# A graph-network layer in fp32 on one core: tile 1 turned on TensorE, HT_hi and HT_lo doubled, and the first tiles reordered

## What is computed

```python
h = jnp.maximum(_layernorm(x, axis=-1), 0.0)                    # x: 50000 x 256
agg = segment_sum(edge_attr_64, dst, 50000)                     # 25000 edges x 64, dst sorted
agg = agg / jnp.maximum(counts, 1.0)[:, None]
combined = jnp.concatenate([agg, h], axis=1)                    # 50000 x 320
out = x + relu(combined @ W1 + b1) @ W2 + b2                    # W1 320 x 512, W2 512 x 256
```

## Time and profile before

| | |
|---|---|
| median of 3 runs | 1362.57 us (1361.99 to 1363.06) |
| the profiled execution's own time | 1361.83 us |
| its span | 1360.0 us |
| busy: TensorE products | 1333.9 us (98%) |
| busy: VectorE | 1194.1 us (88%) |
| busy: ScalarE | 695.4 us (51%) |
| busy: POOL | 539.7 us (40%) |
| chain that ended last | TensorE 95%, VectorE 3%, DMA 1%, POOL 1% |

### The profile page before, as it was taken

One profiled execution on the slowest core, in us unless ns is written; L12 is line 12 of the kernel. 1 busy time (PEld: TensorE's weight loads), 2 busy tenths in 40 slices (PEclk: granted clock), 3 DMA queues, 4 the chain that ended last, 5 costly groups with the idle time before them and its releaser, 6 DMA issues.

```text
span 1360.0 us, 29811 instructions
## 1 busy us (share of the span) xinstructions
PE 1333.9 (98%) x7066; PEld 1118.8 (82%) x7066; DVE 1194.1 (88%) x2961; ACT 695.4 (51%) x1281; POOL 539.7 (40%) x710
## 2 busy tenths in 40 slices
PE   4899999999999999999999999999999999999999
PEld 2688888888888888888888888888888888888887
DVE  5989898988888898989898989898889888989897
ACT  3445555555555454545454545454545454545553
POOL 6333343434343434343434343434343434343431
PEclk9999999999999999999999999999999999999999
DMA  4455555555454545454545464545454545555542
GB/s 112 111 127 120 133 121 130 126 126 130 121 132 120 132 120 133 119 136 115 140 112 143 109 147 107 145 108 143 111 141 112 139 114 137 116 135 118 133 111 74
DMA packets 422724, 168.59 MB, mean 124 GB/s; under 512 B 321188, under 2 KB 422326, under 8 KB 422712
## 3 DMA queue, kind: packets, MB, share of 16 engines
q1 hardware_dynamic: 421720, 167.28, 51.2%
q10 hardware_dynamic: 992, 1.18, 0.3%
HBM read 66.12 MB, written 51.40 MB: 86 GB/s over the span
## 4 chain that ended last, share of the span: by engine, by line
PE 95%; DVE 3%; DMA 1%; POOL 1%; issue 0%; ACT 0%; POOLq 0%; DVEq 0%; SPq 0%
PE P L907 26%; PE P L909 13%; PE P L884 13%; PE P L886 13%; PE P L885 13%; PE P L893 6%; PE P L894 6%; PE PA L873 2%; PE PA L874 2%; DVE H_lo L715 0%; DMA dst_w<-in_dst_dram 0%; DVE OH L813 0%; DVE below L670 0%; DVE stats L645 0%; DVE HT L699 0%
## 5 line engine op out<-in xcount | busy, mean ns | idle before, releaser
L907 PE MATMUL P<-w_both,H_hi 128*128 128x512 f32 x1564 | 557.6, 397 | 1.1 <-DVE H_lo L715 1.0
L596 ACT ACTIVATE H_hi<-P 128x512 fp32r<-128x512 f32 x392 | 233.1, 596 | 513.4 <-PE P L894 513.4
L909 PE MATMUL P<-w_both,H_lo 128*128 128x256 f32 x1564 | 439.6, 281 | 0.0
L715 DVE SCALAR_TENSOR_TENSOR H_lo<-P,H_hi 128x512 fp32r<-128x512 f32 x392 | 268.0, 685 | 113.2 <-ACT H_hi L596 103.2
L907 PEld LDWEIGHTS P<-w_both,H_hi 128*128 128x128 f32 x1564 | 293.7, 188 | 74.8 <-DVE H_lo L715 3.4
L884 PE MATMUL P<-HT_hi,w_hi 128*128 128x512 f32 (+1 forms) x784 | 314.4, 401 | 1.9 <-ACT w_both L610 1.9
L886 PE MATMUL P<-HT_hi,w_lo 128*128 128x512 f32 (+1 forms) x784 | 308.9, 394 | 0.0
L885 PE MATMUL P<-HT_lo,w_hi 128*128 128x512 f32 (+1 forms) x784 | 306.0, 390 | 0.0
L909 PEld LDWEIGHTS P<-w_both,H_lo 128*128 128x128 f32 x1564 | 293.4, 188 | 3.7
L438 POOL TENSOR_TENSOR XB<-X,b_row 128x1024 f32<-128x1024 f32 x98 | 236.8, 2416 | 135.5 <-DVE O L729 135.3
L432 POOL TENSOR_TENSOR E_lo<-ES,E_hi 128x256 fp32r<-128x256 f32 x98 | 73.2, 747 | 400.6 <-ACT E_hi L576 400.6
(11 more groups left out here) (74 smaller groups left out, 1140.0 us busy)
## 6 DMA issues: line engine op xcount, KB each, us to landing
HQ<-HN SPq DMA_DIRECT2D x388, 128.0 KB, 3.1
out_dram<-O SPq DMA_DIRECT2D x97, 512.0 KB, 3.3
X<-in_x_dram SPq DMA_DIRECT2D x96, 512.0 KB, 3.6
ER<-in_edge_attr_dram SPq DMA_DIRECT2D x392, 32.0 KB, 1.8
DT<-table_dram SPq DMA_DIRECT2D x392, 1.0 KB, 1.7
X<-in_x_dram ACTq DMA_DIRECT2D x1, 512.0 KB, 5.0
w_raw<-in_L_gnn_W_dram ACTq DMA_DIRECT2D x4, 128.0 KB, 5.2
w_raw<-in_L_gnn_W_dram SPq DMA_DIRECT2D x2, 256.0 KB, 4.0
```

Of the source, the lines that this page charges most:

```text
L596: act.activation(H1_hi[:, m, nodes(t)], bank(m)[:, nodes(t)], ACT.Relu).then_inc(s_1hi, 1)
L715: dve.scalar_tensor_tensor(out=H1_lo[:, m, nodes(t)], in0=bank(m)[:, nodes(t)], scalar=0.0, in1=H1_hi[:, m, nodes(t)], op0=ALU.max, op1=AL ...
L907: pe.matmul(out_bank(j)[some, :], H1_hi[:, m, rows], w2_both[:, m, :, :].rearrange("p a d -> p (a d)"), start=(m == 0), stop=False)
L909: last = pe.matmul(out_bank(j)[some, 0:D], H1_lo[:, m, rows], w2_both[:, m, 0, :], start=False, stop=(m == CH - 1))
```

## The change

Tile 1 is turned as tile 0 is: TensorE transposes HN of tile 1 into the P2 banks, and SP's move and VectorE's transposes of tile 1 are gone. HT_hi and HT_lo have two buffers, taken by turns. The first-layer products of tile 0 have another order: all w1_hi x HT_hi, then the transposes of tile 1, all w1_lo x HT_hi, the edge means, all w1_hi x HT_lo. POOL computes norm(1) directly behind w1_lo, the parts wb_lo behind the flag's test, norm(2) behind the low part of w2, and each XB of tiles 1, 2 and 3 behind that tile's edges and behind a new wait for its one-hots (`s_oh`). ScalarE normalizes tile 1 ahead of the split of w2 and makes HT_hi of tile 1 ahead of tile 0's means. VectorE tests the flag before `transposed_low(0)` and the statistics of tile 2; the one-hots of tile 3 come before the residuals of tile 1, and `means_low(2)` after the first of them. In `moved` the count of moves is adapted.

```diff
@@ -141,4 +141,4 @@
         HT = sb("HT", [P, CD, TILE])
-        HT_hi = sb("HT_hi", [P, CD, TILE], F32R)
-        HT_lo = sb("HT_lo", [P, CD, TILE], F32R)
+        HT_hi = [sb(f"HT_hi{b}", [P, CD, TILE], F32R) for b in range(2)]
+        HT_lo = [sb(f"HT_lo{b}", [P, CD, TILE], F32R) for b in range(2)]
         QA = sb("QA", [P, TILE], F32R)
@@ -194,3 +194,3 @@
 
-            return P2[c][:] if isinstance(t, int) and t == 0 else HT[:, c, :]
+            return P2[c][:] if isinstance(t, int) and t < 2 else HT[:, c, :]
 
@@ -268,4 +268,4 @@
             if isinstance(t, int):
-                return MOVED * (t // 2 + b)
-            return MOVED // 2 * t + MOVED // 2 * b
+                return MOVED * (t // 2)
+            return MOVED // 2 * t - MOVED // 2 * b
 
@@ -382,3 +382,2 @@
             load_windows(1, 1)
-            move(1, 1)
             load_x(3, 1)
@@ -477,10 +476,3 @@
             pool.tensor_tensor(w1_lo[:], w1_raw[:], w1_hi[:], ALU.subtract).then_inc(s_wlo, 1)
-            pool.wait_ge(s_whi, 3)
-            pool.wait_ge(s_wlo, 1)
-            pool.tensor_tensor(wb_lo[0:DE, :], wa_raw[0:DE, :], wa_hi[0:DE, :], ALU.subtract).then_inc(s_wblo, 1)
-            pool.wait_ge(s_wblo, 1)
-            pool.tensor_tensor(wb_lo[96:P, :], b1_raw[96:P, :], b1_hi[96:P, :], ALU.subtract).then_inc(s_wblo, 1)
-            pool.wait_ge(s_wblo, 2)
             norm(1, 1)
-            norm(2, 0)
             pool.wait_ge(s_start, 1)
@@ -530,2 +522,7 @@
                     pool.wait_ge(s_gout, 16 * i + 16)
+            pool.wait_ge(s_whi, 3)
+            pool.tensor_tensor(wb_lo[0:DE, :], wa_raw[0:DE, :], wa_hi[0:DE, :], ALU.subtract).then_inc(s_wblo, 1)
+            pool.wait_ge(s_wblo, 1)
+            pool.tensor_tensor(wb_lo[96:P, :], b1_raw[96:P, :], b1_hi[96:P, :], ALU.subtract).then_inc(s_wblo, 1)
+            pool.wait_ge(s_wblo, 2)
             edges_scaled(0, 0)
@@ -534,7 +531,10 @@
             pool.tensor_tensor(w2_both[:, :, 1, :], w2_raw[:], w2_both[:, :, 0, :], ALU.subtract).then_inc(s_wlo, 1)
-            residual_in(1, 1)
+            norm(2, 0)
             edges_scaled(1, 1)
             edges_low(1, 1)
+            pool.wait_ge(s_oh, 2 * SUB)
+            residual_in(1, 1)
             edges_scaled(2, 0)
             edges_low(2, 0)
+            pool.wait_ge(s_oh, 3 * SUB)
             residual_in(2, 0)
@@ -543,2 +543,3 @@
             edges_low(3, 1)
+            pool.wait_ge(s_oh, 4 * SUB)
             residual_in(3, 1)
@@ -566,3 +567,3 @@
                     rows, into = X[b][:, j, :], HN[b][:, j, :]
-                    if isinstance(t, int) and t == 0:
+                    if isinstance(t, int) and t < 2:
                         rows = rows.rearrange("p (q c f) -> p q c f", q=QN, c=CD)
@@ -577,7 +578,7 @@
 
-            def transposed_high(t):
-                past(act, s_l1, CH * t)
+            def transposed_high(t, b):
+                past(act, s_l1, CH * (t - 1))
                 for c in range(CD):
                     act.wait_ge(s_th, 2 * t + c + 1)
-                    act.activation(HT_hi[:, c, :], turned(t, c), ACT.Copy).then_inc(s_hhi, 1)
+                    act.activation(HT_hi[b][:, c, :], turned(t, c), ACT.Copy).then_inc(s_hhi, 1)
 
@@ -607,7 +608,8 @@
             layernorm(0, 0)
-            transposed_high(0)
+            transposed_high(0, 0)
+            layernorm(1, 1)
             act.wait_ge(s_w[3], 32)
             act.activation(w2_both[:, :, 0, :], w2_raw[:], ACT.Copy).then_inc(s_whi, 1)
-            layernorm(1, 1)
             edges_high(0, 0)
+            transposed_high(1, 1)
             means_high(0)
@@ -616,3 +618,2 @@
             layernorm(2, 0)
-            transposed_high(1)
             means_high(1)
@@ -620,3 +621,3 @@
             hidden_high(1)
-            transposed_high(2)
+            transposed_high(2, 0)
             means_high(2)
@@ -627,3 +628,3 @@
                     hidden_high(2 * i + h)
-                    transposed_high(2 * i + (h + 1))
+                    transposed_high(2 * i + (h + 1), 1 - h)
                     means_high(2 * i + (h + 1))
@@ -632,3 +633,3 @@
             hidden_high(TILES - 2)
-            transposed_high(TILES - 1)
+            transposed_high(TILES - 1, 1)
             means_high(TILES - 1)
@@ -701,3 +702,3 @@
 
-            def transposed_low(t):
+            def transposed_low(t, b):
                 for c in range(CD):
@@ -705,4 +706,4 @@
                     if c == 0:
-                        past(dve, s_l1, CH * t)
-                    dve.tensor_tensor(HT_lo[:, c, :], turned(t, c), HT_hi[:, c, :], ALU.subtract).then_inc(s_hlo, 1)
+                        past(dve, s_l1, CH * (t - 1))
+                    dve.tensor_tensor(HT_lo[b][:, c, :], turned(t, c), HT_hi[b][:, c, :], ALU.subtract).then_inc(s_hlo, 1)
 
@@ -745,3 +746,3 @@
                     transpose(t + 1, 1 - b, 1)
-                    transposed_low(t + 1)
+                    transposed_low(t + 1, 1 - b)
                 if latest:
@@ -766,6 +767,3 @@
             stat(1, 1, range(SUB))
-            transposed_low(0)
             aggregate(1, 1)
-            stat(2, 0, range(SUB))
-            aggregate(2, 0)
             dve.wait_ge(s_start, 1)
@@ -816,4 +814,8 @@
             dve.wait_ge(s_const, 12)
+            transposed_low(0, 0)
+            stat(2, 0, range(SUB))
+            aggregate(2, 0)
             ends(0, 0)
             onehot(0, 0)
+            transposed_low(1, 1)
             means_low(0)
@@ -823,5 +825,2 @@
             onehot(1, 1)
-            transpose(1, 1, 0)
-            transpose(1, 1, 1)
-            transposed_low(1)
             means_low(1)
@@ -838,10 +837,9 @@
             transpose(2, 0, 1)
-            transposed_low(2)
-            residual(1, 1, 0)
-            residual(1, 1, 1)
-            means_low(2)
-            residual(1, 1, 2)
-            residual(1, 1, 3)
+            transposed_low(2, 0)
             ends(3, 1)
             onehot(3, 1)
+            residual(1, 1, 0)
+            means_low(2)
+            for j in range(1, SUB):
+                residual(1, 1, j)
             with dve.Fori(1, TILES // 2 - 1) as i:
@@ -876,3 +874,3 @@
 
-            def layer1_nodes(t, m):
+            def layer1_nodes(t, b, m):
                 if m == 0:
@@ -883,5 +881,5 @@
                 for c in range(CD):
-                    pe.matmul(bank(m)[:, nodes(t)], w1_hi[:, c, cols], HT_hi[:, c, nodes(t)], start=(c == 0), stop=False)
-                    pe.matmul(bank(m)[:, nodes(t)], w1_hi[:, c, cols], HT_lo[:, c, nodes(t)], start=False, stop=False)
-                    pe.matmul(bank(m)[:, nodes(t)], w1_lo[:, c, cols], HT_hi[:, c, nodes(t)], start=False, stop=False)
+                    pe.matmul(bank(m)[:, nodes(t)], w1_hi[:, c, cols], HT_hi[b][:, c, nodes(t)], start=(c == 0), stop=False)
+                    pe.matmul(bank(m)[:, nodes(t)], w1_hi[:, c, cols], HT_lo[b][:, c, nodes(t)], start=False, stop=False)
+                    pe.matmul(bank(m)[:, nodes(t)], w1_lo[:, c, cols], HT_hi[b][:, c, nodes(t)], start=False, stop=False)
 
@@ -918,3 +916,3 @@
                     if not (isinstance(t, int) and t == 0):
-                        layer1_nodes(t, m)
+                        layer1_nodes(t, b, m)
                     layer1_means(t, m)
@@ -922,2 +920,5 @@
                         edge_means(t + 1, 1 - b)
+                if isinstance(t, int) and t == 0:
+                    pe.wait_ge(s_whi, 5)
+                    pe.wait_ge(s_wlo, 2)
                 layer2(t)
@@ -927,8 +928,11 @@
             pe.wait_ge(s_const, 9)
-            for j in range(SUB):
-                pe.wait_ge(s_ln, j + 1)
-                for c in range(CD):
-                    last = pe.transpose(P2[c][:, j * P:(j + 1) * P], HN[0][:, j, c * P:(c + 1) * P], ident[:])
-                    if j == SUB - 1:
-                        last.then_inc(s_th, 1)
+            def turn(t):
+                for j in range(SUB):
+                    pe.wait_ge(s_ln, SUB * t + j + 1)
+                    for c in range(CD):
+                        last = pe.transpose(P2[c][:, j * P:(j + 1) * P], HN[t][:, j, c * P:(c + 1) * P], ident[:])
+                        if j == SUB - 1:
+                            last.then_inc(s_th, 1)
+
+            turn(0)
             with pe.If(flag != 0):
@@ -941,12 +945,18 @@
             pe.wait_ge(s_whi, 1)
+            for c in range(CD):
+                pe.wait_ge(s_hhi, c + 1)
+                for m in range(CH):
+                    pe.matmul(bank(m)[:], w1_hi[:, c, m * P:(m + 1) * P], HT_hi[0][:, c, :], start=(c == 0), stop=False)
+            pe.wait_ge(s_hlo, 2)
+            turn(1)
             pe.wait_ge(s_wlo, 1)
-            layer1_nodes(0, 0)
-            layer1_nodes(0, 1)
-            layer1_nodes(0, 2)
-            layer1_nodes(0, 3)
+            for c in range(CD):
+                for m in range(CH):
```

(6 more changed lines are left out.)

## The result

The changed kernel takes 1365.13 us (median of 13 runs, 1363.44 to 1366.32), the kernel before, run beside it, 1362.38 (13 runs, 1360.39 to 1364.74): a ratio of 1.0025, 95% interval [1.0017, 1.0033]. It is 2.75 us slower by the medians. The interval lies clear of 1, so it is a small loss, just above the 0.2% (2.7 us) that the prediction calls no difference. The profiled execution took 1366.23 us, with a span of 1364.6, and is near the slow end of its 13 runs.

A forecast was written before the change was run, and what follows sets the result against it. TensorE never waits in the steady loop, so only the first four tiles count. 0.4 us less and 1.6 more turn the profiled 1361.83 into 1363.0; from the median, 1362.57 + 1.2 = 1363.7, range 1357.0 to 1366.4.

The forecast's parts named there:

- The start: Up to S, when tile 0's means products begin on TensorE: S at 32.0 instead of 34.41, a gain of 2.4 us.
- XB(1), X(3), ES(2): POOL's XB(1) waits for one-hot(1) until 37, SP's X(3) goes out at 39.5, 2.8 later, and ES(2) starts at 48.5.
- Layer 2 of tile 1: TensorE starts it at 51.1 as before, behind a new 2.9 us wait; the 2.4 us are given back whole.
- One-hots of tile 3 early and alone, no wait for them: VectorE's one-hots take 0.9 us; TensorE's 2.53 us wait and 1.57 of slow clock go, less about 1 us.
- Moves of tile 3 from 65.8: SP's moves, queued without a pause from X(3), begin at 65.8 instead of 63.01.
- HQ(3) landed, the fourth slice at 72.9: Tile 2's layer 2: landing at 71.1, H_lo at 72.9; TensorE waits 2.7 us, gains 0.4 us against 73.34.
- Clock loss 1.6, bounds 0 and 1.6: Slow TensorE products behind the 2.7 us wait at 70.2 add 1.6 us.
- A fall at 48 to 51 that the later wait swallows: Clock fall behind the wait before tile 1's layer 2, possible; the wait at 70 swallows it, no size added.
- rival 3: Tile 1's transposes keep TensorE's clock low: S = 34.5, no gain at the start, 3.7 us more, 1366.3; chance 0.16.
- Rival 1: The new wait of TensorE before tile 2's fourth slice costs no clock: 1362.2, no difference; chance 0.26.
- Rival 2: Tile 2's windows and HQ(3) arrive about 3 us earlier, in time: 6.5 us less, 1356.1; chance 0.27.
- Rival 4: One-hots meet ES, E_lo or wb_lo instead of XB: at most 0.6 to 1.3 us each on VectorE; no own chance.

The follow-up runs named there:

- experiment 1: The changed kernel with SP issuing the window loads of tile 2 ahead of X(3): 1355.98 us, ratio 0.9962 to the kernel before.
- experiment 2: The changed kernel with XB(1) back right behind POOL's low part of w2, without its wait for one-hots: 1358.93 us, ratio 0.9979 to the kernel before.
- peeled control: The changed kernel with TensorE's steps of tiles 2 and 3 written out ahead of its loop, same work and order: 1363.70 us, ratio 1.0021 to the kernel before.
- filled kernel: The peeled control plus 14 idle TensorE products ahead of the fourth slice of tile 2's layer 2: 1362.25 us, ratio 1.0008 to the kernel before.
- experiment 9: The changed kernel without POOL's wait for tile 1's one-hots ahead of XB(1), its new place kept: 1362.75 us, ratio 1.0015 to the kernel before.
- experiment 4: The kernel before with POOL's XB of tiles 2 and 3 waiting for their one-hots, nothing else: 1359.53 us, ratio 0.9995.
- experiment 10: The changed kernel with nine idle TensorE products ahead of tile 0's transposes: 1363.87 us, ratio 1.0023 to the kernel before.
- experiment 3: The kernel before with two buffers for HT_hi and HT_lo, nothing moved: 1361.03 us, ratio 1.0001.
- experiment 5: Two kernels made from the changed one, the peeled control and the filled kernel: 1363.70 and 1362.25 us.
- experiment 7: Experiment 3 with tile 1 turned on TensorE behind tile 0's 24 products and its move gone, POOL as before: 1362.37 us, ratio 1.0008 to the kernel before.
- experiment 8: Experiment 4 with SP's window loads of tile 2 ahead of the move of tile 1 and X(3): 1364.06 us, ratio 1.0024 to the kernel before.

## Why the prediction was right in its chain and short in its sum

The prediction gave 1363.7 us (1357.0 to 1366.4), 1.4 below what was measured; its own terms, 1362.57 + 1.2, make 1363.8. Its moments stand for a T of 20.50; those of the changed kernel are given here less 1.96.

- **The start.** S was 32.27 for a predicted 32.0, the first product 23.14 for 23.0. Right, gain 2.14 for 2.4.
- **XB(1), X(3), ES(2).** 37.13, 39.63 and 48.56 for 37, 39.5 and 48.5. Right to 0.15 us, and experiments 1 and 2 show that this chain holds TensorE.
- **Layer 2 of tile 1.** 50.89 for 51.1, behind a wait of 2.33 for 2.9. Right.
- **One-hots of tile 3 early and alone, no wait for them.** Right in effect; they too took 1.13 us. QA(2) behind them held TensorE for 0.63 us (63.07), which the wait ahead of the fourth slice swallowed.
- **Moves of tile 3 from 65.8.** 65.77. Right.
- **HQ(3) landed, the fourth slice at 72.9.** First miss, 0.7 us: the transpose began at 71.91, not 71.1, though SP issued on time, and the slice came at 73.56. The step was "its landing 3.2 after it". The landing of the last move took 4.0 us in this execution, but at most 3.2 in the peeled control, the filled kernel and experiment 9 (3.6 in experiment 1), so the row was right as a typical one. The predicted gain of 0.4 became a loss of 0.22.
- **Clock loss 1.6, bounds 0 and 1.6.** Second miss, 0.9 us: 2.47 in the profiled execution. The upper bound was taken from one row. Experiments 2, 4 and 9 lost 1.54 us each, about that row's 1.57; after's fall lasted for eight of the ten pairs. The other row, a wait of 1.60 without a loss, was no safe one either: in experiment 4 the same wait cost clock.
- **A fall at 48 to 51 that the later wait swallows.** Right: behind the wait of 2.33 the clock fell, and TensorE still stood 3.55 us before the fourth slice.

The two misses are terms of the sum that were mis-sized: the landing of the last move, and the clock loss. Together, 0.6 + 0.9 = 1.5, they are what the difference was short: 1.2 was forecast, 2.75 measured. That this fits so well is in part luck, for both sizes are those of one execution, and the medians come from 13 on either side, which differ among themselves by 2.9 and 4.4 us. By the prediction's own classes, slower by over 0.2% had a chance of 0.16 and stood for rival 3; the measured 0.25% falls just into it (the interval covers both sides), though rival 3 is not what happened.

**Rival 1** (no clock loss, 1362.2) has its mechanism in the profiled executions of the control and of experiment 10, where the last wait cost no clock, and the filled kernel leaves no such wait. Its price did not come: rival 1 stands 0.4 below the kernel before, while the filled kernel's 1362.25 stands 1.2 above the 1361.01 beside it, and nearly the same figure is a coincidence of chips. **Rival 2** (loads in time, 1356.1) fell for the changed kernel, since X(3) behind XB(1) is indeed an order and not a rate. Its price was nearly right: where the loads are in time, in experiment 1, the span from T is 7.0 us shorter than before's, for 6.5 predicted, and the median 5.1 below that of the kernel before beside it. That 1355.98 is so close to 1356.1 is chance. **Rival 3** (transposes keep the clock low, S = 34.5) fell, though the slower outcome that it stood for came by another way. Of the changed kernel's first eight products, 0.43 us apart, the first starts at 25.10; eight transposes follow at 28.65, and at 29.92 eight products take 2.09 us, 0.24 apart. The granted clock goes from 0.50 over 0.69 to 1.00 at 30, some 4.5 us after the first product, as without transposes in between (24.47 to 28.87). The rule of the Trainium skill, TensorE: Matmul & The Clock Gate, Part 4: PE-mode transpose, that transposes don't count as busy for the clock, made no difference that this trace shows. **Rival 4** was in the numbers as it was in the text: one-hots(2) and (3) met ES and took 1.13 us, 0.25 more.

How much of the 2.75 us is the clock stays open. In profiled executions whose last long wait cost no clock the spans from T are 1337.7 for before's order (experiment 3) and 1339.3 and 1339.8 for the changed order (control, experiment 10): 1.6 to 2.1 apart. With a fall there in both they are 1339.5 and 1342.1: 2.6 apart. So most of the loss is the order of SP's queue, seen at the fourth slice (51.11 in experiment 3, 52.54 and 53.09 there), which before's own fall hides in its row of 52.84. The prediction counted that fall of 1.57 as a gain of the change, since it stood in the one profiled execution; in an execution of the old order without it, as in experiment 3, the gain is not there.

## What to carry to other kernels

When a stage leaves a queue, look at what that queue does next: the place it frees is worth something only if the loads that others wait for move into it, and here two lines of SP's order turned 2.75 us lost into 5.1 won. Hold a bulky operation back from its neighbour only after following who waits for its result: XB(1) was kept off 0.88 us of one-hots and held up everything behind X(3). And align two traces on a common event past the set-up before comparing them, or 1.96 us that come and go by themselves are taken for the change.

## What the runs showed of the hardware

- **The clock falls in some executions, and the wait's length alone doesn't decide it.** In the profiled executions it fell behind a wait of 1.60 us (experiment 4, at 34.55), of 2.23, 2.26 and 2.86 (experiments 4, 2, 9), of 2.31 to 2.33 before layer 2 of tile 1 (after, both kernels of experiment 5, experiment 10), of 2.34 and 2.53 (experiment 7), 2.53 (before), 3.55 (after) and 5.00 (experiment 8). It did not fall behind 1.60 (before, experiments 3 and 8), 2.53 (experiment 3), 3.29 and 3.60 (control, experiment 10). At the fourth slice a fall cost 1.54 us in three kernels and 2.47 in one. In experiment 7 the products from 67.67 on stand 0.43 us apart up to 71.09.
- **VectorE beside POOL.** The subtraction `reach` of the set-up, with two inputs in SBUF, took 1.59 us beside POOL's XB(0) in the changed kernel's execution (row 14.57 above) and 0.71 in before's, where XB(0) was nearly over; the one-hots took 0.88 us alone, 1.13 beside ES and 2.98 to 3.57 beside XB.
- **A store's issue can hold its queue.** Behind the moves of tile 3 it took 2.14 us (70.51 on SP), in experiment 1 1.68, in the control and experiments 4 and 9 each time 0.63. In the two executions with the long issue the last move landed late as well, 4.0 and 3.6 us after its issue instead of 3.2; which is the cause of which isn't shown.
